# One product of states with C for each unit of a selective scan on GpSimd, instead of two halves

## The chip, the cores and the metric
The kernel runs on one core of one Trainium2 chip. The metric is the device time of one execution in microseconds (us). The engines work side by side, each through its own list of instructions in order, and wait for each other by semaphores: TensorE (PE, with its weight loads as PEld), VectorE (DVE), ScalarE (ACT), GpSimd (POOL) and SyncE (SP), which issues the DMAs.

## The reference
An adaLN block over 16 batches of 512 tokens and 256 channels: a modulated layer norm, a two-way Mamba layer, a gated residual, then a ternary feed-forward network. What matters here is the selective scan of the Mamba layer, with E = 512 channels and N = 64 states in each of two directions:

```python
def step(h, inp):
    xt, dtt, Bt, Ct = inp
    dA = jnp.exp(dtt[:, :, None] * A)
    h = dA * h + (dtt * xt)[:, :, None] * Bt[:, None, :]
    y = jnp.einsum('ben,bn->be', h, Ct)
    return (h, y)
```

Its output gets `xc * Dp` added, is multiplied by `silu(z)`, and goes through `W_out`. Two layer norms and the network of four weight layers follow.

## The kernel before
**Units.** A batch is a body of 128 units; the bodies are "pre", "first", "mid" (a loop of 14), "last" and "tail", and the middle three scan. A unit is one direction, one group of 128 channels (a pass of 16 units) and 4 of the 64 states. Its state tile is 128 partitions (32 channels times 4 states) by 4 blocks of 512 time steps: 2,048 columns, in a ring of four (`STATE_RING`). A half of it is two blocks, 1,024 columns; halves are counted as q = 2 * unit + h.

**The way of a unit.** ScalarE writes the decays exp(dt * A) into the state tile (L1083), once the sum of the unit four before has freed the slot. The drives, u * B, come into PSUM (`driven`, two halves) in one of two ways: for even units DVE multiplies `ud_rep` with B rows spread by TensorE (L1272, spread at L873); for odd units ScalarE and POOL make `v_sb` (L1096, L1380) and TensorE transposes it (L883), each half when the scan two halves before has left its bank. DVE scans each half in place (L1283) and counts `scanned`. POOL multiplies the states with the row of C (`c_rep`, a ring of two), in place, in `read` (L1313), and counts `was_read`: two for a unit. TensorE sums the four blocks over the states into `y_ps` (L905) when both are counted, and counts `summed`. SP loads the next row of C (`load_c`, L553) when `was_read` says that the unit two before is done.

**The order on the engines.** Each engine's list is written unit by unit. DVE: scan, scan, then, if the next unit is even, its two drives, then side steps. POOL: every second unit a `make_v`, then the two `read`s, then side steps. TensorE at an even unit: the first half's drive of the next unit, the second half's drive and the spread; the sum of the unit before stands ahead of the second drive in the `CROWDED` units, ahead of both where a pass ends (unit % 16 == 0), and otherwise behind them; then side steps. At an odd unit: the sum of the unit before and side steps. SP's list has the loads of C with those of weights (`wq_sb`, `wp_sb`) and of `ud_rep` behind them in one queue.

**Side steps** are the other parts of the block for the same, the next and the previous batch, set to unit numbers in fixed tables. Those that the text names: on POOL "o_rstd" (unit 10), "pre2" (14), "n_rstd" (20), "glu00" and "glu01" (35, 36; L1364), "ua" and "ub" of p1 (43, 44; L1368), "x_rstd" and "h_rstd" (66, 73), "add0" (76), "glu10" and "glu11" (86, 87), "ua" and "ub" of next (111, 112). On DVE, with both inputs in SBUF: "mix" (unit 15, L1238), "rest" (40 in p1 and 108 in next: L1253, then L1255), "dt" (42 and 110, L1259), "x_scale" and "x_shift" (68 and 69, L1231 and L1234). Here p1 is the second direction of this batch, next the first direction of the next one. DVE's scans and drives take one of their inputs from PSUM.

Of the kernel before, what the change touches and what calls it, by code (L numbers as in the profile page):

```python
# [7 lines left out]
ALU = mybir.AluOpType  # L8
ACT = mybir.ActivationFunctionType

P = 128
BATCH, T, D = 16, 512, 256
# [12 lines left out]
HALVES = 2 * UNITS  # L25
NG, NN, EG = 16, 4, 32
JC = P // EG
PASSES = 2 * EC
DRIVE_RING, STATE_RING, ROW_RING, V_RING, V_AHEAD, POOL_AHEAD = 2, 4, 2, 2, 5, 3
# [185 lines left out]
def adaln_kernel(nc, x, win, wxp, wdt, wout, f1, h1, h2, w3, cols, rows, c_t, wmod, consts, spread_rows, out):  # L215
    ctx = ExitStack()
    with ctx:
        def sb(name, shape, dt=F32):
            return ctx.enter_context(nc.sbuf_tensor(name, shape, dt))

        def sem(name):
            return ctx.enter_context(nc.semaphore(name))
# [32 lines left out]
        state = sb("state", [P, STATE_RING, JC, T])  # L255
        c_rep = sb("c_rep", [P, ROW_RING, T])
# [60 lines left out]
        b_spread, decayed, dve_driven, pe_driven, v_made, v_pooled, scanned, was_read, summed = (  # L317
            sem(n) for n in ("b_spread", "decayed", "dve_driven", "pe_driven", "v_made", "v_pooled", "scanned", "was_read", "summed"))
        c_in = [sem(f"c_in{i}") for i in range(ROW_RING)]
# [61 lines left out]
        def of_body(at, per_body, index):  # L381

            return at.b * per_body + index
# [15 lines left out]
        def c_loaded(at, unit):  # L399

            return of_body(at, 16 * UNITS // ROW_RING, 16 * (unit // ROW_RING + 1))
# [902 lines left out]
        def _(pool):  # L1304
            pool.sem_inc(was_read, 2 * ROW_RING)

            def read(at, q):
                unit, h = q // 2, q % 2
                pool.wait_ge(scanned, of_body(at, HALVES, q + 1) + DRIVE_RING)
                if h == 0:  # L1310
                    pool.wait_ge(c_in[unit % ROW_RING], c_loaded(at, unit))
                part = state[:, unit % STATE_RING, 2 * h:2 * h + 2]
                pool.tensor_tensor(part, part, c_rep[:, unit % ROW_RING, :].unsqueeze(1).to_broadcast([P, 2, T]),  # L1313
                                   ALU.mult).then_inc(was_read, 1)

            def step(at, part, name):
                done = pool_side.sem
# [52 lines left out]
            def side(at, unit):  # L1370
                for s, part, name, _ in POOL_SIDE:
                    if s == unit and at.has(part):
                        step(at, part, name)

            def make_v(at, unit):
                nth, g = unit % UNITS // NG, unit % NG
                pool.wait_ge(pe_driven, v_free(at, unit))
                if g == 1:
                    pool.wait_ge(act_side.sem, act_side.done(at, "o0" if nth else "next", f"UT{nth}"))
                pool.tensor_tensor(v_sb[:, unit // 2 % V_RING, TT - 1].rearrange("p j e n -> p (j e) n"),  # L1380
                                   u_t[:, nth % 2, TT - 1, :].unsqueeze(2).to_broadcast([P, P, NN]),
                                   b_t[:, nth // EC, TT - 1, NN * g:NN * (g + 1)].unsqueeze(1).to_broadcast([P, P, NN]),
                                   ALU.mult).then_inc(v_pooled, 1)

            def body(at):
                for unit in range(UNITS):
                    ahead = unit + POOL_AHEAD
                    if unit % 2 == 0 and (at.kind in SCAN_PARTS if ahead < UNITS else at.has("next")):
                        make_v(at, ahead)
                    if at.kind in SCAN_PARTS:  # L1390
                        read(at, 2 * unit)
                        read(at, 2 * unit + 1)
                    side(at, unit)

            bodies(pool, body)


# [49 lines left out]
```

## Time and profile before
| | |
|---|---|
| median of 3 runs | 12745.45 us (12720.19 to 12750.62) |
| profiled execution, its own time | 12767.88 us |
| its span | 12766.1 us |
| mean granted TensorE clock | 0.887 |
| DVE busy | 11968.4 us, 94% |
| POOL busy | 11345.7 us, 89% |
| ACT busy | 10843.4 us, 85% |
| PE busy | 10393.6 us, 81% |

The profile is one execution. The span runs from its first to its last instruction. Busy time counts an instruction from start to end, also where it is held up inside; idle time before an instruction is put down to the one that released it, its "releaser". A line such as L1313 is that of the kernel's source.

### The profile page before, as it was taken

To read this page: it belongs to the slowest core of one execution; us is meant where nothing else is said; L and a number is where in the kernel's file an instruction comes from. 1 tells how busy PE (TensorE), PEld (TensorE's weight loads), DVE (VectorE), ACT (ScalarE), POOL (GpSimd) and SP (SyncE) were. 2 spreads that over 40 slices of the span, in tenths; PEclk is the share of its full clock that TensorE was granted. 3 is DMA by queue.
4 is the path that set the end of the run, shared out by engine and by line. 5 is a ranking of instruction groups with operands and counts; after the bars stand their busy time and mean duration, and the time that the engine had idled before them with its cause. 6 is when DMAs were issued, how large, how long until landed. Compare 5 with 4: busy or idle time off the path is not lost.

```text
span 12766.1 us, 179504 instructions
## 1 busy us (share of the span) xinstructions
PE 10393.6 (81%) x51484; PEld 5920.3 (46%) x51484; DVE 11968.4 (94%) x7080; ACT 10843.4 (85%) x23460; POOL 11345.7 (89%) x5924
## 2 busy tenths in 40 slices
PE   5678878888888888878888888887878878788887
PEld 2334544445454444544445444454544445444445
DVE  5999999999999999999999999999999999999992
ACT  5788888888888898888888888888888988888882
POOL 4899999899998999999998998999989999999992
PEclk7778988889898998988989898998989989889888
DMA  2223333333333333433333333333333333333332
GB/s 89 83 87 111 119 112 126 122 108 117 110 127 115 117 125 106 130 111 121 122 113 115 112 125 121 109 120 107 128 111 119 123 108 127 112 124 121 111 111 96
DMA packets 610266, 1459.04 MB, mean 114 GB/s; under 512 B 68928, under 2 KB 110032, under 8 KB 604672
## 3 DMA queue, kind: packets, MB, share of 16 engines
q1 hardware_dynamic: 609152, 1446.18, 35.0%
q8 instruction: 456, 7.47, 0.2%
q14 instruction: 658, 5.39, 0.1%
HBM read 1355.09 MB, written 90.83 MB: 113 GB/s over the span
## 4 chain that ended last, share of the span: by engine, by line
issue 26%; PE 25%; ACT 19%; DVE 16%; POOL 10%; DMA 1%; DVEq 0%; POOLq 0%; SPq 0%; ACTq 0%
DVE state L1283 11%; POOL state L1313 8%; PE driven L883 7%; ACT state L1083 7%; ACT v_sb L1096 6%; PE q_ps L838 5%; PE y_ps L905 4%; DVE driven L1272 3%; PE p_ps L746 2%; PE q_ps L825 2%; PE b_ps L873 1%; PE p_ps L754 1%; ACT L1083 1%; PE p_ps L770 1%; PE p_ps L761 1%
## 5 line engine op out<-in xcount | busy, mean ns | idle before, releaser
L1313 POOL TENSOR_TENSOR state<-state,c_rep 128x1024 f32<-128x1024 f32 x4096 | 9682.4, 2393 | 971.5 <-DVE state L1283 965.2
L1283 DVE TENSOR_TENSOR_SCAN state<-state,driven 128x1024 f32<-128x1024 f32 x4096 | 9089.4, 2267 | 298.0 <-PE driven L883 280.5
L1083 ACT ACTIVATE state<-ud_rep,cols_sb 128x512 f32<-128x512 f32 x8192 | 5212.5, 710 | 3.1 <-PE y_ps L905 0.6
L1096 ACT ACTIVATE v_sb<-u_t,b_t 128x128 f32<-128x128 f32 x12288 | 4062.0, 505 | 1136.5 <-PE driven L883 1133.4
L883 PE MATMUL driven<-consts_sb,v_sb 128*128 128x128 f32 x16384 | 2713.9, 320 | 1486.3 <-DVE state L1283 1463.2
L883 PEld LDWEIGHTS driven<-consts_sb,v_sb 128*128 128x128 f32 x16384 | 2184.5, 164 | 2692.0 <-DVE state L1283 2001.2
L905 PE MATMUL y_ps<-state,consts_sb 128*32 128x512 f32 x16384 | 2455.2, 677 | 289.2 <-POOL state L1313 287.1
L1272 DVE TENSOR_TENSOR driven<-ud_rep,b_ps 128x1024 f32<-128x1024 f32 x2048 | 2389.6, 1212 | 18.1 <-DMA ud_rep<-ud_rows 18.1
L838 PE MATMUL q_ps<-hid,wq_sb 128*128 128x256 f32 x7936 | 2081.0, 408 | 139.8 <-ACT hid L1061 76.4
L838 PEld LDWEIGHTS q_ps<-hid,wq_sb 128*128 128x128 f32 x7936 | 1498.0, 199 | 1016.3 <-issue 818.1
L1380 POOL TENSOR_TENSOR v_sb<-u_t,b_t 128x512 f32<-128x512 f32 x1024 | 1083.5, 1058 | 36.4 <-issue 23.5
L905 PEld LDWEIGHTS y_ps<-state,consts_sb 128*32 128x32 f32 x16384 | 346.6, 114 | 1213.9 <-POOL state L1313 675.2
L873 PE MATMUL b_ps<-b_parts,onehot 32*128 32x512 f32 x1024 | 574.2, 561 | 0.0
L825 PE MATMUL q_ps<-xn_q,wq_sb 128*128 128x256 f32 x1984 | 508.6, 400 | 44.9 <-ACT hid L1051 22.4
L746 PE MATMUL p_ps<-x_t,wp_sb 128*128 128x512 f32 x1024 | 503.6, 615 | 37.3 <-ACT xc L989 24.2
L754 PE MATMUL p_ps<-u_pad,dt_sb 128*128 128x512 f32 x1024 | 514.3, 626 | 20.0 <-ACT u_pad L985 19.9
L825 PEld LDWEIGHTS q_ps<-xn_q,wq_sb 128*128 128x128 f32 x1984 | 365.8, 194 | 221.1 <-issue 99.2
L848 PE MATMUL q_ps<-wq_sb,hid 128*128 128x256 f32 x992 | 282.0, 434 | 68.3 <-ACT hid L1066 64.6
L1061 ACT ACTIVATE hid<-q_ps,cols_sb 128x256 f32<-128x256 f32 x496 | 223.4, 450 | 129.7 <-PE q_ps L838 129.5
L746 PEld LDWEIGHTS p_ps<-x_t,wp_sb 128*128 128x128 f32 x1024 | 189.3, 194 | 269.9 <-issue 185.0
L754 PEld LDWEIGHTS p_ps<-u_pad,dt_sb 128*128 128x128 f32 x1024 | 188.1, 197 | 269.2 <-issue 213.7
L873 PEld LDWEIGHTS b_ps<-b_parts,onehot 32*128 32x128 f32 x1024 | 208.5, 204 | 210.4 <-issue 210.4
(141 smaller groups left out, 5585.8 us busy)
## 6 DMA issues: line engine op xcount, KB each, us to landing
c_rep<-bc_rows SPq DMA_DIRECT2D x2048, 256.0 KB, 3.0
ud_rep<-ud_rows SPq DMA_DIRECT2D x512, 512.0 KB, 4.0
wq_sb<-in_h SPq DMA_DIRECT2D x512, 512.0 KB, 3.9
wq_sb<-in_f SPq DMA_DIRECT2D x128, 512.0 KB, 4.2
wp_sb<-in_win SPq DMA_DIRECT2D x64, 512.0 KB, 4.1
dt_sb<-conv_taps SPq DMA_DIRECT2D x32, 1024.0 KB, 5.2
ud_rows<-u_pad SPq DMA_DIRECT2D x128, 256.0 KB, 3.4
ud_rows<-dt_sb SPq DMA_DIRECT2D x128, 256.0 KB, 3.5
```

Source lines behind the costliest of these rows:

```text
L746: mm = pe.matmul(p_ps[:], wp_sb[:, m, k, :], x_t[:, k, :], start=(k == 0), stop=(k == DC - 1))
L825: mm = pe.matmul(bank[:, which * TH:(which + 1) * TH], w[:, m % 2, which, k, :], n_t[:, k, i * TH:(i + 1) * TH], start=(k == 0), stop=(k = ...
L838: mm = pe.matmul(bank[:, 0:TH], w[:, k, :], src[:, k, :], start=(k == 0), stop=(k == HC - 1))
L873: pe.matmul(b_ps[:], onehot[k, g % quarter, :], b_parts[d][k, :], start=True, stop=True).then_inc(b_spread, 1)
L883: mm = pe.transpose(driven[:, q % DRIVE_RING, j % 2, tt * P:(tt + 1) * P], v_sb[:, unit // 2 % V_RING, tt, j].rearrange("p e n -> p (e n)" ...
L905: mm = pe.matmul(y_ps[EG * j:EG * (j + 1), :], over_nn, state[:, k % STATE_RING, j, :], start=False, stop=(g == NG - 1))
L1083: ins = act.activation(state[:, unit % STATE_RING, j, :], ud_rep[:, nth % 2, j, 1, :], ACT.Exp, scale=a_neg[:, d, c, j, g:g + 1])
L1096: ins = act.activation(v_sb[:, unit // 2 % V_RING, tt, :, :, n].rearrange("p j e -> p (j e)"), u_t[:, nth % 2, tt, :], ACT.Identity, scale ...
L1272: dve.tensor_tensor(driven[:, h], u_rows(unit)[:, 2 * h:2 * h + 2], b_ps[:].unsqueeze(1).to_broadcast([P, 2, T]), ALU.mult).then_inc(dve_d ...
L1283: dve.tensor_tensor_scan(flat, flat, driven[:, q % DRIVE_RING].rearrange("p j t -> p (j t)"), 0.0, ALU.mult, ALU.add).then_inc(scanned, 1)
L1313: pool.tensor_tensor(part, part, c_rep[:, unit % ROW_RING, :].unsqueeze(1).to_broadcast([P, 2, T]), ALU.mult).then_inc(was_read, 1)
L1380: pool.tensor_tensor(v_sb[:, unit // 2 % V_RING, TT - 1].rearrange("p j e n -> p (j e) n"), u_t[:, nth % 2, TT - 1, :].unsqueeze(2).to_bro ...
```

## The change
`read` is called once for each unit. It waits until both halves are scanned, then for the row of C, multiplies all four blocks in one operation of 2,048 elements in each partition, and counts `was_read` by two. The values that the others wait for stay as they are.

```diff
-            def read(at, q):
-                unit, h = q // 2, q % 2
-                pool.wait_ge(scanned, of_body(at, HALVES, q + 1) + DRIVE_RING)
-                if h == 0:
-                    pool.wait_ge(c_in[unit % ROW_RING], c_loaded(at, unit))
-                part = state[:, unit % STATE_RING, 2 * h:2 * h + 2]
-                pool.tensor_tensor(part, part, c_rep[:, unit % ROW_RING, :].unsqueeze(1).to_broadcast([P, 2, T]),
-                                   ALU.mult).then_inc(was_read, 1)
+            def read(at, unit):
+                pool.wait_ge(scanned, of_body(at, HALVES, 2 * unit + 2) + DRIVE_RING)
+                pool.wait_ge(c_in[unit % ROW_RING], c_loaded(at, unit))
+                part = state[:, unit % STATE_RING]
+                pool.tensor_tensor(part, part, c_rep[:, unit % ROW_RING, :].unsqueeze(1).to_broadcast([P, JC, T]),
+                                   ALU.mult).then_inc(was_read, 2)
...
                     if at.kind in SCAN_PARTS:
-                        read(at, 2 * unit)
-                        read(at, 2 * unit + 1)
+                        read(at, unit)
                     side(at, unit)
```

## Rows read from the trace of the kernel before
**Rows 1.** The page: span, and busy time of each engine.
```profile
span 12766.1 us, 179504 instructions
PE 10393.6 (81%) x51484; PEld 5920.3 (46%) x51484; DVE 11968.4 (94%) x7080; ACT 10843.4 (85%) x23460; POOL 11345.7 (89%) x5924
```
**Rows 2.** The page's groups: shapes, count | busy, mean ns | idle before, releaser.
```profile
L1313 POOL TENSOR_TENSOR state<-state,c_rep 128x1024 f32<-128x1024 f32 x4096 | 9682.4, 2393 | 971.5 <-DVE state L1283 965.2
L1283 DVE TENSOR_TENSOR_SCAN state<-state,driven 128x1024 f32<-128x1024 f32 x4096 | 9089.4, 2267 | 298.0 <-PE driven L883 280.5
...
L905 PE MATMUL y_ps<-state,consts_sb 128*32 128x512 f32 x16384 | 2455.2, 677 | 289.2 <-POOL state L1313 287.1
L1272 DVE TENSOR_TENSOR driven<-ud_rep,b_ps 128x1024 f32<-128x1024 f32 x2048 | 2389.6, 1212 | 18.1 <-DMA ud_rep<-ud_rows 18.1
```
**Rows 3.** The waits, whole span: us in total, times, longest.
```profile
POOL state L1313 <- DVE state L1283: 965.2, 806, 7.9
...
PEld y_ps L905 <- POOL state L1313: 675.2, 613, 5.5
...
PE y_ps L905 <- POOL state L1313: 287.1, 230, 4.8
DVE state L1283 <- PE driven L883: 280.5, 373, 3.2
```
**Rows 4.** Timeline of DVE, 5387 to 5410 us: start, us, instruction.
```profile
5395.74 8.81 DVE L1283 TENSOR_TENSOR_SCAN state<-state,driven 128x1024 f32<-128x1024 f32 x4
5404.47 2.33 DVE L1272 TENSOR_TENSOR driven<-ud_rep,b_ps 128x1024 f32<-128x1024 f32 x2
```
**Rows 5.** Timeline of POOL, the same stretch; idle before in brackets.
```profile
5396.54 1.03 POOL L1380 TENSOR_TENSOR v_sb<-u_t,b_t 128x512 f32<-128x512 f32 x1
5398.18 9.35 POOL L1313 TENSOR_TENSOR state<-state,c_rep 128x1024 f32<-128x1024 f32 x4 [0.61 <-DVE state L1283]
```
**Rows 6.** Groups of POOL by shape: small and half-size operations.
```profile
L1356 POOL TENSOR_TENSOR x_q<-x_q,hid 128x512 f32<-128x512 f32 x32 | 41.0, 1282 | 160.6 <-DVE hid L1243 160.6
...
L1335 POOL TENSOR_TENSOR small<-u_pad,small 128x4 f32<-128x4 f32 x64 | 13.1, 205 | 5.0
```
**Rows 7.** Single lines of DVE: ns min/median/max, first and last start.
```profile
L1255 DVE TENSOR_TENSOR dt_sb<-dt_sb,u_pad x32: 2292/4332/4348, 138.2 to 12009.3; 128x2048 f32<-128x2048 f32 x32
...
L1259 DVE TENSOR_TENSOR dt_sb<-dt_sb,sz x32: 2291/2574/4021, 140.6 to 12024.5; 128x2048 f32<-128x2048 f32 x32
...
L1234 DVE TENSOR_TENSOR xa<-xa,mod_p x16: 1226/1525/3439, 51.1 to 11416.4; 128x1024 f32<-128x1024 f32 x16
...
L1238 DVE TENSOR_TENSOR o_sb<-o_sb,mod_q x16: 1226/6342/6650, 1023.6 to 12536.9; 128x1024 f32<-128x1024 f32 x16
```
**Rows 8.** Timeline of DVE at unit 40, 5041 to 5052 us.
```profile
5042.34 2.60 DVE L1253 SCALAR_TENSOR_TENSOR u_pad<-sz,u_pad 128x2048 f32<-128x2048 f32 x1
5044.97 4.34 DVE L1255 TENSOR_TENSOR dt_sb<-dt_sb,u_pad 128x2048 f32<-128x2048 f32 x1
```
**Rows 9.** Timeline of POOL in the same stretch.
```profile
5040.40 6.76 POOL L1313 TENSOR_TENSOR state<-state,c_rep 128x1024 f32<-128x1024 f32 x2 [0.63 <-DVE state L1283]
```
**Rows 10.** Timelines of POOL and of DVE at unit 108, 5441 to 5456 us.
```profile
5443.06 4.72 POOL L1313 TENSOR_TENSOR state<-state,c_rep 128x1024 f32<-128x1024 f32 x2 [1.06 <-DVE state L1283]
...
5447.69 2.29 DVE L1253 SCALAR_TENSOR_TENSOR u_pad<-sz,u_pad 128x2048 f32<-128x2048 f32 x1 [2.61 <-ACT sz L1021]
```
**Rows 11.** Timeline of all engines at units 88 to 91, 5325 to 5343 us.
```profile
5326.63 2.39 POOL L1364 TENSOR_TENSOR hid<-hid 128x1024 f32<-128x1024 f32 x1
...
5329.96 9.35 POOL L1313 TENSOR_TENSOR state<-state,c_rep 128x1024 f32<-128x1024 f32 x4
...
5334.71 1.06 PE L905 MATMUL y_ps<-state,consts_sb 128*32 128x512 f32 x8 [2.22 <-POOL state L1313]
...
5342.02 2.29 DVE L1283 TENSOR_TENSOR_SCAN state<-state,driven 128x1024 f32<-128x1024 f32 x1 [3.05 <-PE driven L883]
```
**Rows 12.** A step of POOL that each batch has once: its first and last start.
```profile
L1346 POOL TENSOR_TENSOR xn_q<-xn_q,mod_q x16: 2355/2364/2387, 965.9 to 12524.3; 128x1024 f32<-128x1024 f32 x16
```

## The prediction
> **What bounds the kernel now.** I began with the page. VectorE (DVE) is busy for 11,968 of 12,766 us, GpSimd (POOL) for 11,346 [rows 1]. Both run a chain of operations unit by unit: DVE's scan takes 2.27 us for half a unit, POOL's product with C 2.39 us, and DVE also builds the drive of every second unit [rows 2]. So DVE sets the pace, with POOL close behind. Then the waits: POOL waited 965 us for scans, 806 times. TensorE (PE), which sums the products (L905), found one missing 613 times at a weight load and 230 times at a matmul, and DVE waited 280 us for the drives that TensorE makes behind those sums [rows 3]. POOL is thus mostly early, and where it is late it reaches DVE through TensorE's order.
>
> The reader should see the rhythm next. Four scans and two drives begin again every 10.97 us (5384.77 is 10.97 before the 5395.74 shown, and 5406.71 after it; of these one stands) [rows 4]. In the same stretch POOL's v takes 1.03, four products 9.35, and 0.61 is left waiting for a scan [rows 5]. It starts the first half of a unit 0.16 us after that half's scan, and ends 2.68 after the second scan. That is the commonest picture: I lined the products up with the scans over the middle bodies, and about half of the 128 units look so; some 40 have POOL over 1 us late, behind its side work. A body lasts (12524.3 - 965.9) / 15 = 770.6 us [rows 12].
>
> **The duration of the joint product.** An operation of 4 elements took 205 ns and one of 512 took 1,282, against 2,370 or so for 1,024 [rows 2, 6]. From 512 to 1,024 the slope is 1.09 us, which leaves 1.28 - 1.09 = 0.19 as the fixed part, the same as the small one shows. Two products back to back take 4.65 us; the joint one should take 4.65 - 0.19 = 4.46 (bound on the other side: 4.65, nothing saved). POOL saves at most 2,048 x 0.19 = 389 us of its own time.
>
> **When it ends.** It starts after the second scan, so where POOL was early it ends 0.16 + 4.46 = 4.62 us after that scan instead of 2.68: 1.94 later. For the odd unit, which follows at once, it is 4.71 instead of 2.99. Where POOL was late already, it ends 0.19 earlier per unit. Behind the waiting instruction on POOL stand v and the side steps (rstd, glu, ua, ub, add), which start 1.9 us later too. SP's load of the next C row waits for the same semaphore, and SP's weight loads stand behind it. That C load itself is hidden: 3 us of landing against the 4.46 of the product between. POOL keeps the rhythm: 2 x 4.46 + 1.03 is 9.95 of 10.97.
>
> **Part one: DVE blocked by the longer operation.** DVE operations with both inputs in SBUF run unevenly: L1255 takes 2.29 alone but 4.33 at the median; L1234 1.23 and 1.53; L1238 1.23 and 6.34; L1259 2.29, 2.57 and up to 4.02 [rows 7]. The timeline shows why. POOL's second half of unit 40 and L1253 want the same thing; the pair of products takes 6.76 instead of 4.70, and L1255 ends 2.2 us after POOL's end [rows 8, 9]. One engine waits until the other's operation is over. The scans and drives read one input from PSUM and stay at their length. The trace has no POOL operation of over 2.4 us of work here, so what a longer one does is bounded: 0 if DVE gets a turn inside it, 4.46 - 2.37 = 2.1 us per meeting if it does not. I take the second, since no row shows a turn inside.
> The Trainium skill, "SBUF — State Buffer", section "SBUF: two separate sides", says that a DVE operation with two SBUF inputs and a GpSimd operation lock one pair of ports, whichever starts first, for the whole instruction. By that rule it is the 2.1 us, by the lower bound nothing. The trace agrees as far as 1,024 elements go; L1238's 6.34 is more than one POOL operation, which the page does not say.
> Per body, from the positions:
> - L1255 in p1: L1253 starts as the scan ends, before POOL, and now ends unhindered (-0.3), then the whole product, then L1255: +1.8 in all.
> - L1253 in next: it waits 2.61 us for ScalarE, to 5447.69, while POOL's two products ran to 5447.78 [rows 10]. The joint one runs from 5445.2 to 5449.7: +1.9.
> - L1259 in next: ready 0.8 us after the scan; waited for the half product to 1.86, will wait for the whole to 3.8: +1.9. In p1 it starts before POOL: -0.3.
> - L1234: ready after the two drives, 2.3 us after the scan; the joint product holds it to 4.6: +2.1.
> - L1231 between -0.4 and +2.0, depending on where the late POOL stands: I take +0.5.
> - L1238 is held by a POOL that is late already: -0.2; between -4 (it gets its turn between two longer operations) and +1.
> Sum 7.8 us a body, bounds 3 and 10. With about 15.5 bodies: 121 us.
>
> **Part two: sums that come later, and drives behind them.** TensorE's order puts the sum of an odd unit ahead of a drive in the crowded units. Most sums have room: in the crowded stretches TensorE arrives 2 to 4 us after the product. The exception shows best at unit 88: POOL does read 86, glu, read 87, glu, v and read 88 without a break, ending at 5334.64; the sum waited 2.22 us for it, and DVE then 3.05 for the drive behind it (2.2 over the middle bodies) [rows 11]. The chain starts from a unit where POOL was early: 1.94 later, less 2 x 0.19 over two joint products, gives 1.5 us, all on DVE. Similar bursts: rstd at 20 and at 73 (with SP's late f10 load behind it at 76), ua and ub at 43 and 44, and the sums at the pass ends 64, 112 and 0, which had 0.2 of margin. I put 1 us on each of the first three and 1 on the ends together: 1.5 + 4 = 5.5. I take off 1 for places where DVE waits for TensorE or ScalarE anyway: 4.5 us a body, 70 us. Bounds: 0, and 230 matmul waits x 1.7 = 391 us.
>
> **Sum.** 121 + 70 = 191 us. Profiled span 12,766 + 191 = 12,957; 1.8 us lie around the span (12,767.88 in all), and the median is 22.4 below that run: 12,935. Its own range: port 3 to 10, TensorE 0 to 10 us a body, so +50 to +315: 12,795 to 13,060.
>
> **The rivals.**
> - *Faster: POOL's backlog shrinks.* POOL is late in some 40 units of 128. If its 0.19 there all came back through TensorE, that is 7.6 us a body, and if L1238 also gets its turn between two operations, 4 more: (7.6 + 4) x 15.5 = 180, so 12,565. For it: POOL on the path at L905. Against: bursts start from units in which POOL was early, and two joint products regain only 0.38 of 1.94. It decides if backlogs last over ten units (1.94 / 0.19). Chance 0.08.
> - *No change.* DVE gets its turn within a long operation, and the 1.94 us are slack everywhere: 12,745. For it: half the units have 1 us or more between drive and scan. Against: rows 8 and 11. 0.09.
> - *Much slower: every exposed sum costs.* If the 230 waits each grow by 1.7 and reach DVE, 391 + 121: 13,257. Against: DVE waited only 280 us for drives at 373 places, so most waits of TensorE for POOL are absorbed. 0.07.
> The forecast keeps 0.76.
>
> **Range and chances.** The range takes the forecast's own bounds and a little of the two neighbours: 12,770 to 13,070. About 0.3% (38 us) is what a measurement tells from no change. Slower: 0.76 + 0.07 + 0.01 = 0.84; same 0.08; faster 0.08.
>
> **What would show it.** In the profile after: POOL's product x2048 at 4.46 to 4.5 us; L1234's median near 3.6, L1259's maximum near 6, L1255 near 6.4 in p1; the wait of DVE for the drives grown from 280 by some 70 us; PE and PEld waits for POOL well up. If the DVE rows of [rows 7] stay as they are, part one is wrong. If the DVE waits do not grow, part two is. A joint product under 4.3 us, or L1238 down to 2 us, would break the sum from below; a new wait of ScalarE for the sums or of POOL for C rows, of which the page of before lists none, from above.

## The result, and the profile after
The changed kernel takes 12,897.5 us (median of 4 runs, 12,890.7 to 12,904.7) against 12,746.6: 1.0123 times as long, 95% interval 1.0105 to 1.0140. The forecast was 12,935, slower, with a range of 12,770 to 13,070. The profiled execution took 12,904.68 us, its span is 136.8 us longer than that of before, and the comparison below is between these two spans.

The page after, its groups, to be held against [rows 2]:
```profile
span 12902.9 us, 176560 instructions
...
PE 10239.6 (79%) x51484; PEld 5841.2 (45%) x51484; DVE 12007.6 (93%) x7080; ACT 10863.7 (84%) x23460; POOL 11086.5 (86%) x3876
...
L1311 POOL TENSOR_TENSOR state<-state,c_rep 128x2048 f32<-128x2048 f32 x2048 | 9401.4, 4601 | 1396.0 <-DVE state L1283 1276.2
L1283 DVE TENSOR_TENSOR_SCAN state<-state,driven 128x1024 f32<-128x1024 f32 x4096 | 9094.4, 2269 | 339.6 <-PE driven L883 321.0
...
L905 PE MATMUL y_ps<-state,consts_sb 128*32 128x512 f32 x16384 | 2418.9, 665 | 1036.2 <-POOL state L1311 1034.1
```
POOL is busy 281 us less with the product, and waits 425 us more before it. The scans did not get slower. DVE is busy 39 us more than before and idle 98 us more; together they are the 137 us. TensorE's matmul wait for a product is 1,034 us instead of 287, yet DVE's wait for drives rose only from 280 to 321 [rows 3]. So most of TensorE's new waiting did not reach DVE through the drives, and DVE's loss must be looked for elsewhere too. Three of its waits before (us in total, times, longest):
```profile
DVE xc L1202 <- PE y_ps L905: 12.9, 30, 3.4
...
DVE dt_sb L1259 <- ACT sz L1024: 11.2, 14, 0.8
...
DVE dt_sb L1262 <- POOL u_pad L1368: 4.8, 1, 4.8
```
And its waits after:
```profile
DVE state L1283 <- PE driven L883: 321.0, 414, 4.1
...
DVE dt_sb L1262 <- POOL u_pad L1366: 45.6, 30, 4.8
DVE xc L1202 <- PE y_ps L905: 41.5, 42, 6.3
```
The last two are the news. L1262 is the memset "cut" (side steps of units 45 and 113), which waits for POOL's ub: 45.6 us where it was 4.8, which is 1.4 us at each of 29 new places. L1202 multiplies a pass's output and waits for its last sum: 41.5 us where it was 12.9. Most of that growth stands at unit 16, right behind mix (1.6 us in each middle body, none before). The wait of L1259 for ScalarE, 11.2 us before, is gone.

The single lines of DVE with two SBUF inputs (ns min/median/max), against [rows 7]:
```profile
L1253 DVE SCALAR_TENSOR_TENSOR u_pad<-sz,u_pad x32: 2265/2269/4320, 139.1 to 12138.8; 128x2048 f32<-128x2048 f32 x32
...
L1255 DVE TENSOR_TENSOR dt_sb<-dt_sb,u_pad x32: 2293/6516/6526, 141.4 to 12141.1; 128x2048 f32<-128x2048 f32 x32
...
L1259 DVE TENSOR_TENSOR dt_sb<-dt_sb,sz x32: 2259/2262/2294, 143.8 to 12158.5; 128x2048 f32<-128x2048 f32 x32
...
L1231 DVE TENSOR_TENSOR xa<-xa,mod_p x16: 1225/1300/2579, 50.9 to 11527.8; 128x1024 f32<-128x1024 f32 x16
...
L1234 DVE TENSOR_TENSOR xa<-xa,mod_p x16: 1224/4450/4472, 52.1 to 11535.6; 128x1024 f32<-128x1024 f32 x16
...
L1238 DVE TENSOR_TENSOR o_sb<-o_sb,mod_q x16: 1226/2558/7707, 1031.5 to 12670.1; 128x1024 f32<-128x1024 f32 x16
```
L1255 and L1234 grew by 2.2 and 2.9 us at the median. L1253 takes 4.31 at unit 108 in the mean of the middle bodies, where it took 2.29. L1238 lost 3.8 of its 6.3, and L1259 all that held it. These six lines (L1231, L1234, L1238, L1253, L1255, L1259) are busy for 466 us in all, against 435 before.

For where in a body this happens, the starts of the scans were read from the traces and the lengths of the units averaged over the 14 middle bodies (us from one unit's first scan to the next's). All units not listed sum to the same within 2.3 us:

| units | before | after | late halves | port halves | run halves | and from 84 | DVE first x3, joint | DVE first x5, joint | late joint |
|---|---|---|---|---|---|---|---|---|---|
| 15, 16 | 17.3 | 17.5 | 18.0 | 17.3 | 17.4 | 17.2 | 17.5 | 17.4 | 15.6 |
| 24, 25 | 11.0 | 11.7 | 12.9 | 11.7 | 11.8 | 11.0 | 12.1 | 11.7 | 11.0 |
| 40 | 11.3 | 13.1 | 10.9 | 12.3 | 13.1 | 13.1 | 8.9 | 8.9 | 11.4 |
| 42 | 6.9 | 6.6 | 9.1 | 6.6 | 7.9 | 7.9 | 11.3 | 10.5 | 6.9 |
| 45, 46 | 11.4 | 13.2 | 13.1 | 13.3 | 11.3 | 11.3 | 12.8 | 12.6 | 11.3 |
| 68, 69 | 15.8 | 17.6 | 15.9 | 15.4 | 17.7 | 17.8 | 14.5 | 14.3 | 15.9 |
| 78 | 4.9 | 6.5 | 6.4 | 5.7 | 4.9 | 5.2 | 6.3 | 7.1 | 4.6 |
| 89, 90 | 13.3 | 15.2 | 15.4 | 15.5 | 15.3 | 14.1 | 15.7 | 15.6 | 12.4 |
| 108 | 11.6 | 13.6 | 13.7 | 12.6 | 13.6 | 13.6 | 11.6 | 11.6 | 11.7 |
| 110 | 9.2 | 6.6 | 6.6 | 6.6 | 7.9 | 7.9 | 11.3 | 7.9 | 9.2 |
| 113, 114 | 12.0 | 12.2 | 12.7 | 12.2 | 11.2 | 11.6 | 11.0 | 12.3 | 11.8 |
| others | 649.0 | 648.3 | 650.7 | 648.7 | 647.4 | 647.7 | 651.3 | 648.3 | 648.6 |
| body | 773.6 | 782.3 | 785.2 | 777.8 | 779.5 | 778.4 | 784.3 | 778.2 | 770.1 |

The loss of 8.7 us a body stands at a few places. Units 40, 68-69 and 108 lose 5.6 together: there DVE meets the joint product. Units 24-25, 45-46, 78 and 89-90 lose 6.0: there a late product counts. Unit 110 gives 2.6 back. At units 15 and 16 two changes cancel, which their sum hides: unit 15 became 2.1 shorter, as mix is held less, and unit 16 became 2.3 longer, most of it the wait for the pass output.

DVE and then POOL at unit 40 of a middle body (start, us, instruction), against [rows 8, 9]:
```profile
5100.83 2.27 DVE L1253 SCALAR_TENSOR_TENSOR u_pad<-sz,u_pad 128x2048 f32<-128x2048 f32 x1
5103.13 6.52 DVE L1255 TENSOR_TENSOR dt_sb<-dt_sb,u_pad 128x2048 f32<-128x2048 f32 x1
```
```profile
5101.13 6.37 POOL L1311 TENSOR_TENSOR state<-state,c_rep 128x2048 f32<-128x2048 f32 x1 [1.15 <-DVE state L1283]
```
L1253 comes first and takes 2.27, with no 0.3 lost. POOL's product, issued at 5101.13, is done at 5107.50, 4.40 after L1253's end. L1255 is done 2.15 after that. So here each engine waited until the other's whole instruction was over, and the one that had started first was served first. The Trainium skill's rule that was weighed in the prediction (the page "SBUF — State Buffer", section "SBUF: two separate sides") is borne out by these rows for 2,048 elements.

### The profile page after: what moved, and what is told of

Read it like the earlier page. It is cut to its first block, busy times and chain, and to the rows that moved or that the text cites. A ratio compares the mean times of both kernels' runs of the same rounds, so it can differ in the third digit from the quotient of the medians.

```text
span 12902.9 us, 176560 instructions
## 1 busy us (share of the span) xinstructions
PE 10239.6 (79%) x51484; PEld 5841.2 (45%) x51484; DVE 12007.6 (93%) x7080; ACT 10863.7 (84%) x23460; POOL 11086.5 (86%) x3876
## 4 chain that ended last, share of the span: by engine, by line
PE 25%; issue 25%; ACT 20%; DVE 16%; POOL 11%; DMA 1%; DVEq 0%; SPq 0%; POOLq 0%; ACTq 0%
DVE state L1283 12%; POOL state L1311 9%; ACT state L1083 7%; PE driven L883 7%; ACT v_sb L1096 6%; PE q_ps L838 4%; PE y_ps L905 4%; DVE driven L1272 3%; PE q_ps L825 2%; PE p_ps L746 2%; PE p_ps L754 1%; PE b_ps L873 1%; ACT L1083 1%; ACT hid L1066 1%; PE p_ps L770 1%
## 5 line engine op out<-in xcount | busy, mean ns | idle before, releaser
L1311 POOL TENSOR_TENSOR state<-state,c_rep 128x2048 f32<-128x2048 f32 x2048 | 9401.4, 4601 | 1396.0 <-DVE state L1283 1276.2
L883 PE MATMUL driven<-consts_sb,v_sb 128*128 128x128 f32 x16384 | 2611.6, 313 | 1161.4 <-DVE state L1283 1146.9
L905 PE MATMUL y_ps<-state,consts_sb 128*32 128x512 f32 x16384 | 2418.9, 665 | 1036.2 <-POOL state L1311 1034.1
L883 PEld LDWEIGHTS driven<-consts_sb,v_sb 128*128 128x128 f32 x16384 | 2125.3, 160 | 2320.0 <-DVE state L1283 1602.2
L1272 DVE TENSOR_TENSOR driven<-ud_rep,b_ps 128x1024 f32<-128x1024 f32 x2048 | 2390.1, 1213 | 17.8 <-DMA ud_rep<-ud_rows 17.8
L1378 POOL TENSOR_TENSOR v_sb<-u_t,b_t 128x512 f32<-128x512 f32 x1024 | 1098.5, 1073 | 12.8 <-ACT u_t L1009 12.8
L754 PE MATMUL p_ps<-u_pad,dt_sb 128*128 128x512 f32 x1024 | 501.2, 612 | 17.5 <-ACT u_pad L985 17.5
L746 PE MATMUL p_ps<-x_t,wp_sb 128*128 128x512 f32 x1024 | 502.1, 613 | 15.2 <-ACT sz L1029 10.6
```

Source lines behind the costliest of these rows:

```text
L746: mm = pe.matmul(p_ps[:], wp_sb[:, m, k, :], x_t[:, k, :], start=(k == 0), stop=(k == DC - 1))
L883: mm = pe.transpose(driven[:, q % DRIVE_RING, j % 2, tt * P:(tt + 1) * P], v_sb[:, unit // 2 % V_RING, tt, j].rearrange("p e n -> p (e n)" ...
L905: mm = pe.matmul(y_ps[EG * j:EG * (j + 1), :], over_nn, state[:, k % STATE_RING, j, :], start=False, stop=(g == NG - 1))
L1272: dve.tensor_tensor(driven[:, h], u_rows(unit)[:, 2 * h:2 * h + 2], b_ps[:].unsqueeze(1).to_broadcast([P, 2, T]), ALU.mult).then_inc(dve_d ...
```

## The experiments
Each is built on the same two kernels; times are medians, ratios against runs of the kernel before on the same chip. Between the sets of runs the kernel before had medians from 12,746.6 to 12,757.0, so a difference of some 10 us between two experiments is not told from noise. In most of them `read` can do either form for each unit:
```diff
+                if unit in HALVED:
+                    for h in range(2):
+                        pool.wait_ge(scanned, of_body(at, HALVES, 2 * unit + h + 1) + DRIVE_RING)
...
+                        product(at, unit, h)
+                    return
```

**Only the wait: late_halves.** Halves of 1,024, both behind both scans.
```diff
+                pool.wait_ge(scanned, of_body(at, HALVES, 2 * unit + 2) + DRIVE_RING)
+                pool.wait_ge(c_in[unit % ROW_RING], c_loaded(at, unit))
+                product(at, unit, 0)
+                product(at, unit, 1)
```


> Two products of 1,024 elements again, but both wait for both scans, so it has the change's wait without its length. If the length of POOL's operation is what holds DVE's two-SBUF-input operations, DVE gets its turn between the halves: unit 40 is back near 11.3 us (13.1 after the change), the median of x_shift's L1234 back near 1.5 us (4.45), while the later products still cost at units 45, 78 and 89. Then the time is near the kernel before + 5 us a body = 12,825 us. If the later start alone does it all, L1234 and L1255 stay long and the time is 12,900 or more.

Measured: 12,938.6 us, ratio 1.0154 (1.0136 to 1.0173): slower than the change itself. Half of the expectation held. Unit 40 is at 10.9 us and L1234 (ns min/median/max) is
```profile
L1234 DVE TENSOR_TENSOR xa<-xa,mod_p x16: 1224/2395/2441, 50.4 to 11573.8; 128x1024 f32<-128x1024 f32 x16
```
so 2.05 of the 2.93 us by which L1234 grew are the length of POOL's instruction; the other 0.87 stay and go with its late start. At unit 108 L1253 is held as long as in the changed kernel (4.32 and 4.31 in the mean): there the late start is enough. In all, the six lines are busy for 434 us here, as before the change (435), and the kernel is still the slowest of all: the sum was missed by 114 us. Units 24-25, 42, 45-46, 78, 89-90 and 108 pay for the wait alone, and without the joint form POOL does not get its time per unit back. The wait is the costly half of this change; the joint operation, given the wait, is worth 12,939 - 12,898 = 41 us.

**Halves where DVE meets POOL: port_halves.** `HALVED = (40, 69, 108)`.

> The joint product everywhere but at units 40, 69 and 108, where DVE's rest and x_shift meet it; there the old halves with the old waits. If DVE is held for the whole length of the joint product, these three units give back 1.9 + 2.9 + 2.0 = 6.8 us a body, some 105 us: 12,793. If the loss lies in the later sums alone, three units of 128 change nothing: 12,890.

Measured: 12,835.6 us, ratio 1.0074 (1.0056 to 1.0093). It gives back 62 us of the 105 expected. Unit 40 keeps 1.0 of its loss and 108 another 1.0. The halves remove the hold behind one product, but the joint products around them still move when POOL and DVE meet. Of the 4.5 us a body that came back, 4.0 stand at the three places themselves; unit 78 gives 0.8 more, and others take 0.3. So two fifths of the loss go with these three units. The halves there also end earlier than a joint product; that DVE is held is seen from L1234, 2.22 us in the mean of the middle bodies where it was 4.29.

**Halves at the units with a side step: burst_halves.** `HALVED = (10, 20, 35, 36, 43, 44, 66, 73, 76, 86, 87, 111, 112)`.

> The joint product everywhere but at the 13 units in which POOL has a side step behind the product (rstd, glu, ua, ub, add), where a burst of lateness starts; none of them is 40, 69 or 108. If the burst starts 1.9 us later through the joint product and reaches DVE through TensorE's sums, units 25, 45, 46, 78, 89, 90 and 113 give back about 6 us a body, 90 us: 12,808. If holding DVE is the whole cost, nothing moves: 12,898.

Measured: 12,895.2 us, ratio 1.0116 (1.0096 to 1.0136): nothing came back in sum. By the second hypothesis in the expectation, holding would be the whole cost. The trace says that the experiment missed its aim: the product of unit 43 still ended 4.7 us after its scan (2.6 before), that of 73 4.8 (2.7). An odd unit follows an even one at once, and if the even one is joint, POOL hands its 1.9 us on, whatever form the next has. And the sum hides moves in both directions: against the changed kernel, unit 15 became 1.8 us shorter and units 24-25 0.7, while 68-69 became 1.5 longer, since L1231 is now held too (3.47 us in the mean, 1.56 after the change).

**Both: both_halves.** The 16 units of the two sets.

> Halves at both sets of units, 16 of 128, joint in the other 112. If the two causes are separate they add: 12,898 - 105 - 90 = 12,703, below the kernel before, since what the change gained at units 68 and 110 stays. If the two are one and the same, or the gains are lost with the halves, it is no better than the kernel before, 12,746.

Measured: 12,826.8 us, ratio 1.0065 (1.0043 to 1.0087): 9 us better than port_halves alone, not 90, and not clear of noise; the same flaw.

**Halves in whole runs: run_halves.** To mend it, the units ahead of the bursts as well.
```diff
+            HALVED = (*range(42, 49), *range(72, 80), *range(85, 92), *range(110, 115))
```


> The joint product everywhere but in four whole runs of units, 42 to 48, 72 to 79, 85 to 91 and 110 to 114, which have the old halves: not only the units with a side step on POOL, but those ahead of them, so that a burst starts from an early POOL. 40, 69 and 108 stay joint. If products that end later cost through TensorE, units 45, 46, 78, 89, 90 and 113 go back to their times before and 5.5 us a body come back: 12,898 - 85 = 12,813. If the lateness at these units is not what DVE waits for, it stays at 12,895, as with halves at 13 single units.

Measured: 12,861.7 us, ratio 1.0090 (1.0069 to 1.0111): 36 us come back of the 85 expected. Units 45-46 return from 13.2 to 11.3 and 78 from 6.5 to 4.9, both to their times before; DVE's wait for ub, 45.6 us after the change, is 4.8 again, once, as before. Units 89-90 did not return, and 42 and 110 lose 1.3 each against the changed kernel, since L1259 is held by a half product again (3.5 us in the mean, 2.27 after the change).

**A run that begins at an even unit: run_halves_84.** The third run began at an odd unit, behind the joint product of 84.
```diff
+            HALVED = (*range(18, 28), *range(42, 49), *range(72, 80), *range(84, 92), *range(110, 115))
```


> As the run with four runs of halves, but the third begins at the even unit 84 instead of 85, and a fifth, 18 to 27, is added. In the run before, the joint product of 84 handed its lateness on: the product of 86 ended 4.1 us after its scan (2.7 before the change) and that of 88 8.1 (6.7). If that is why units 89 and 90 stayed at 15.3 us, they go back to 13.3 and the product of 88 to 6.7, and units 24 and 25 from 11.7 to 11.0: 2.7 us a body, 12,862 - 41 = 12,821. If units 89 and 90 are held by something else, they stay at 15.3 and the time is some 12,850.

Measured: 12,835.7 us, ratio 1.0072 (1.0049 to 1.0096): 26 us better than run_halves, of the 41 expected. Units 24-25 are back at 11.0. Units 89-90 fell from 15.3 to 14.1, and the product of 88 from 8.1 to 7.3 us behind its scan (6.7 before): a product that ends 1.4 us late had cost DVE 2.0 there, one of 0.6 costs 0.8. The rest of the lateness still comes in from the joint product of 83, which ends 4.9 us after its scan and not 3.0.

**DVE ahead of the joint product: joint_dve_first.** The changed kernel, POOL waiting for one DVE step more at three units.
```diff
+                    if h == h_waits and at.has(part):
+                        pool.wait_ge(dve_side.sem, dve_side.done(at, part, step_name))
...
+            DVE_FIRST = {40: ('p1', 'rest', 0), 69: ('next', 'x_shift', 0), 108: ('next', 'rest', 0)}
```


> The changed kernel, with POOL's joint product waiting at units 40 and 108 for rest and at 69 for x_shift. If DVE loses there because POOL's operation holds it, unit 40 falls from 13.1 to about 9 us, unit 69 from 11 to 8 and unit 108 from 13.6 to about 10.5, some 10 us a body, 155 us, of which the products that come 3 to 5 us later give back a part through TensorE: 12,770. If only the lateness of the sums counts, it is slower than 12,898.

Measured: 12,918.2 us, ratio 1.0132 (1.0110 to 1.0155). That is 21 us slower than the change, where 12,770 was expected. Units 40 and 69 fell as forecast, by 4.2 and 3.2 us, and unit 108 by 2.0 of the 3.1 forecast. But units 42 and 110 rose by 4.7 each. So the time alone would speak for the second hypothesis, that only late sums count, and the rows speak against it. There stands L1259 (ns min/median/max, and what it waited for):
```profile
L1259 DVE TENSOR_TENSOR dt_sb<-dt_sb,sz x32: 2269/4064/6181, 139.9 to 12173.2; 128x2048 f32<-128x2048 f32 x32
its engine sat idle before it (us, times) until:
  ACT sz L1024: 83.9, 30
```
L1259 needs ScalarE's logarithm, which needs L1253. While DVE was held at 40 and 108, ScalarE had time to finish it, and L1259 went ahead of POOL. With DVE quicker there, L1259 is ready after POOL has begun, and is held in its turn. Of the 4.7 us, 1.7 are L1259 being held (4.00 us in the mean, 2.27 after the change) and 2.8 the wait for the logarithm in front of it, which the earlier hold had hidden. So a part of the hold moved by two units, and behind it a wait came to light.

**And at dt too: joint_dve_first_5.** `42: ('p1', 'dt', 0)` and `110: ('next', 'dt', 0)` are added.

> The changed kernel with POOL's joint product waiting for DVE at five units: 40 and 108 (rest), 69 (x_shift), and now 42 and 110 (dt), where the run with three had moved the loss (+4.7 us each, L1259 at 4.0). L1259 goes back to 2.3 us: 1.7 x 32 = 55 us, and its wait for ScalarE's logarithm stays. Expected 12,865 if holding DVE is what the +4.7 is, so that the change's loss is then almost all later sums; 12,918 or more if POOL's longer waits at 42 and 110 pass on in full.

Measured: 12,823.8 us, ratio 1.0057 (1.0036 to 1.0078), 94 us below the run with three, where 53 were expected. L1234, L1253, L1255 and L1259 are now at their unhindered times; the last is
```profile
L1259 DVE TENSOR_TENSOR dt_sb<-dt_sb,sz 128x2048 f32<-128x2048 f32 x32 | 73.3, 2291 | 74.5 <-ACT sz L1024 74.4
```
The six lines are busy for 309 us in all, against 466 after the change and 435 before. And still the kernel is 0.6% (72 us) slower than before, so holding is not the whole of the loss. The waits for later products are about as long as in the changed kernel: against before, DVE waits 49 us more for the drives, 39 for the cut and 33 for the pass outputs (40, 41 and 29 in the changed kernel). The 72 us are no measure of that share, since POOL's five waits have a price of their own: of the 157 us by which the six lines became shorter only 74 reached the time. L1259, which waited for nothing in the changed kernel, now waits 74 us for the logarithm. Unit 42 is still at 10.5 us. Of the 6.1 us a body against the run with three, 4.2 stand at units 42 and 110; the rest is scattered, and TensorE's mean granted clock was 0.907 here against 0.890 there. Whether the clock is a part of it is open.

**The kernel before, with DVE first: dve_first.** Halves everywhere; POOL's first half waits for mix at 15, its second for rest at 40 and for dt at 110.

> The kernel before, halves everywhere, and POOL's product waits for one DVE step with two SBUF inputs at three units: the first half at 15 for mix, the second at 40 for rest and at 110 for dt. If DVE is held by POOL's operations there, L1238 falls from 6.3 to 1.2 us, L1255 from 4.3 to 2.3 in p1 and L1259 from 4.0 to 2.3 in next; part of mix comes back as a wait of the pass's output for a later sum at unit 16. Together 5 to 6 us a body, 85 us: 12,665. If the long DVE times are not POOL's doing, they stay and the time is 12,751 or more.

Measured: 12,723.1 us, ratio 0.9975 (0.9966 to 0.9985). The holding is real in the kernel before as well: L1238's wait is gone, from 6.34 at the median (ns min/median/max):
```profile
L1238 DVE TENSOR_TENSOR o_sb<-o_sb,mod_q x16: 1217/1218/1225, 1019.4 to 12495.1; 128x1024 f32<-128x1024 f32 x16
```
But the gain is 2.5 us a body, not 5 to 6, and the time is 58 us above the 12,665 expected. Unit 15 becomes 4.4 us shorter and unit 16 3.5 longer, waiting for a product that now comes later; unit 40 gains 1.7 and unit 42 loses 2.3; unit 110 gains 1.7.

**Joint only where POOL is late: late_joint.**
```diff
+            HALVED = tuple(u for u in range(UNITS) if u not in (11, 12, 13, 21, 22, 23, 24, 37, 45, 46, 47, 67, 74, 75, 77, 87, 88, 89, 90, 113, 114))
```


> The joint product only at the 21 units of a body at which POOL in the kernel before arrives when both scans are done or nearly so; the old halves elsewhere. There the joint product waits for nothing new. If the change loses only by starting and ending later than it could, this kernel loses nothing and may keep the 0.15 us of each joint product where a burst reaches DVE: 12,700 to 12,750. If a longer POOL operation costs in itself wherever it stands, it is 21/128 of the way to the change, 12,775.

Measured: 12,708.6 us, ratio 0.9959 (0.9944 to 0.9974): faster than both kernels. The joint operations themselves are as long as in the changed kernel, 4.55 us (L1334 is the joint product in this source; ns min/median/max):
```profile
L1334 POOL TENSOR_TENSOR state<-state,c_rep x336: 4514/4554/4602, 235.3 to 12382.8; 128x2048 f32<-128x2048 f32 x168
```
DVE's wait for drives, 280 before, is
```profile
DVE state L1283 <- PE driven L883: 252.8, 355, 3.2
```
The joint form costs nothing where it waits for nothing, and there its saving reaches DVE, at 89-90 (12.4 against 13.3) and 78 (4.6 against 4.9). But half of the gain, 1.7 of 3.5 us a body, comes from mix at 15-16, whose L1238 is 3.36 us in the mean (5.31 before): it was let in after the first POOL operation in 13 of 16 batches (4 before), and what decides that is open. Unit 15 keeps its halves here and its product ends 7.3 us after the second scan, not 8.6 as in the changed kernel, so unit 16 does not take the gain back. A gain of this size is not sure to come with the same edit elsewhere.

**Both of these: late_joint_dve_first.**

> Both edits of the two kernels before this one. If they touch different places they add: 12,665 less 0 to 45 us. If the later products after POOL's waits at 15, 40 and 110 eat it, no better than the kernel before.

Measured: 12,695.0 us, ratio 0.9951 (0.9935 to 0.9967), which is above all of the 12,620 to 12,665 expected. The interval overlaps that of late_joint; whether the three waits add to it is open.

**Two of the three waits: late_joint_two_first.**

> Joint at the 21 late units, DVE first at 15 (mix) and 110 (dt), not at 40, where going first only moved the loss to unit 42 (-1.9 and +2.3). Expected a little under the run with all three waits: 12,670 to 12,690. If the waits at 15 and 110 gain nothing on top of the 21 joint products, 12,709.

Measured: 12,722.2 us, ratio 0.9975 (0.9965 to 0.9985). Not the 12,670 to 12,690 expected, and not better than without: the interval overlaps that of late_joint too. Against late_joint, unit 110 gained 1.7; unit 15 gained 2.4 and unit 16 gave back 3.2.

## Why the prediction was right, and where not
The direction, the range and the two causes were right. That the number came out as near as it did is in part luck: the part for held DVE operations was put four times too high, and the part for later products too low, and the two errors run against each other (121 + 70 = 191 us forecast; 39 us more busy and 98 us more idle, together 137, in the profile).
- *The duration of the joint product*: 4.46 was forecast, the median is 4.554 and the mean 4.601. The 4.65 of the prediction is twice the distance from one start to the next (2.33 us); from the start of the first half to the end of the second it was 4.70 at the median. So 0.14 us is saved per unit, not 0.19, which is also what POOL's busy time says: 281 us over 2,048 units.
- *When it ends*: right. Where POOL was early, the products of even units end 4.8 us after the second scan (2.7 before) and those of odd ones 4.7 to 4.9 (3.0), some 0.15 to 0.2 later than forecast, by the longer product.
- *DVE held by the longer operation*: the mechanism is right (L1255 in p1 took 6.52, forecast 6.4; late_halves takes L1234 back by 2 us), the term was mis-sized: 121 us against 31, which is the growth of the six lines' busy time from 435 to 466 us. That is 2.0 us a body, below the lower bound of 3. Right were the +1.8 for L1255 in p1 (unit 40: +1.8) and the +1.9 for L1253 in next (unit 108: +2.0). Four terms missed. The +1.9 for L1259 in next came out as a gain of 2.6 at unit 110, because the term was worked out line by line with each line's readiness fixed, while a hold at 108 makes ScalarE's logarithm ready by 110. L1238 was put at -0.2 and became 1.7 shorter in the mean, inside its bounds of -4 and +1, but unit 16 took that back. L1231 was put at +0.5 and came out at -0.7. L1234 cost 2.9 at its median and was forecast at 2.1.
- *Later sums and drives behind them*: 70 us forecast. DVE's own idle time grew by 98 us: 40 for the drives, 41 for the cut, 29 for the pass outputs, less 11 in front of L1259. The forecast put all 70 on the drives and traced the bursts at 43-44 and 111-112 to TensorE. The drives came to 40, and those two bursts reach DVE directly: the cut waits for POOL's ub. The prediction listed ua and ub as standing behind the product and did not ask who waits for them. Most of the 29 for the pass outputs stands at unit 16: DVE comes there 2.1 us earlier, as mix is held less, and the product of unit 15 ends 8.6 us after its second scan, not 6.9.
- *The rivals*: "no change" and "much slower" fall by the measurement. "Faster" had a right condition that the change does not meet: it needs a POOL that is late before the product. Only a kernel that has the joint form at such units alone (21 of 128 were tried) and keeps the halves elsewhere gets it (0.9959).
- How the 151 us divide between the two parts is not shown. With POOL waiting for DVE at five units 74 us come back, and with halves in five runs of units 62; but each of these edits also adds waits or holds of its own (at L1259 in both), so neither number is the share of one cause.
- *Not in the prediction*: TensorE's mean granted clock rose from 0.887 to 0.901, and its 51,484 matmuls were busy for 10,240 us instead of 10,394. Whether this hid a part of the loss was not tested.

## What to carry to other kernels
Joining two operations of a follower engine moves its start to the later of two releases: here it was cheap only where the follower was already late, and the trace says where that is. Before a shared resource is held longer, list every instruction that meets it and let their ready times move too, since a hold in one place can remove the next one, and removing it can bring that one back. And for each step that stands behind the changed instruction, follow its own waiter, not only the main chain's.

## What the runs showed of the hardware
A DVE operation with both inputs in SBUF and a GpSimd product exclude each other by whole instructions: a product of 4.55 us holds L1234 (1.22 alone) up to 4.47, and L1253 held the product, which then took 6.37. DVE's scans and drives, with one input from PSUM, stayed at 2.27 and 1.21 us beside it. Who is served next when both are waiting is not settled by who began to wait first. In the kernel before, L1238 was passed over by POOL in 11 of 16 batches (5.8 to 6.7 us: the rest of one operation, a whole half product and v) and let in after the first operation in 4 (3.0 to 3.3). In the changed kernel, at the same place, it was let in after the first in 11 (2.1 to 2.6) and passed over in 4 (7.3 to 7.7). What decides that is open.
The joint product of 2,048 elements took 4.50 us at the least, against 2.33 for 1,024.
